# Post-LN two-layer kernel on one core: batch 0's second-layer inputs moved into the first phase's last batch, one value product moved into the first pass, the tail split by tiles

## What is computed

```python
x = _layernorm(x + _L0_attn_ref(x, Wq, bq, Wk, bk, Wv, bv, Wo))
x = _layernorm(x + _L0_ffn_ref(x, select_weight, select_mean_diff, ...))
x = _layernorm(x + _L1_attn_ref(x, Wq, Wk, Wv, Wo, bo))
x = _layernorm(x + _L1_ffn_ref(x, G, gate_w, up_w, down_w, lora_A, lora_B))

def _L1_attn_ref(x, Wq, Wk, Wv, Wo, bo):
    q, k, v = split_heads(x @ Wq), split_heads(x @ Wk), split_heads(x @ Wv)
    weights = softmax(einsum('bhqd,bhkd->bhqk', q, k) / sqrt(hd))
    ctx = einsum('bhqk,bhkd->bhqd', weights, v)
    ...
```

## Time and profile before

| | us |
|---|---|
| median of 3 runs | 739.39 |
| lowest and highest | 736.17 and 750.09 |
| the profiled execution | 738.66 |
| its span | 736.8 |
| mean granted clock of TensorE | 0.968 |
| busy: PE, DVE, ACT, POOL | 697.5, 508.7, 404.1, 106.1 |

### The profile page before, as it was taken

One profiled execution on the slowest core, in us unless ns is written; L12 is line 12 of the kernel. 1 busy time (PEld: TensorE's weight loads), 2 busy tenths in 40 slices (PEclk: granted clock), 3 DMA queues, 4 the chain that ended last, 5 costly groups with the idle time before them and its releaser, 6 DMA issues.

```text
span 736.8 us, 11487 instructions
## 1 busy us (share of the span) xinstructions
PE 697.5 (95%) x4080; PEld 483.0 (66%) x4080; DVE 508.7 (69%) x1158; ACT 404.1 (55%) x745; POOL 106.1 (14%) x116
## 2 busy tenths in 40 slices
PE   8999999999999999997899998999999999999975
PEld 5768987798878887896544543555464555546654
DVE  4666556765577656774888797869779787783463
ACT  5574356643665377552137765766548566475531
POOL 0202320132103322232202000200001000000010
PEclk9999999999999999999789999999999999999996
DMA  8300000010000020005504600252004510000000
GB/s 337 149 1 1 29 1 1 0 47 0 0 0 0 12 79 1 4 1 87 123 4 76 99 3 0 41 91 45 2 1 78 90 37 2 2 1 30 1 30 28
DMA packets 13997, 28.31 MB, mean 38 GB/s; under 512 B 2612, under 2 KB 3452, under 8 KB 13820
## 3 DMA queue, kind: packets, MB, share of 16 engines
q1 hardware_dynamic: 13084, 26.10, 14.8%
q10 hardware_dynamic: 864, 1.57, 1.3%
HBM read 12.60 MB, written 2.10 MB: 20 GB/s over the span
## 4 chain that ended last, share of the span: by engine, by line
PE 68%; DVE 18%; issue 7%; ACT 2%; DMA 2%; POOL 1%; ACTq 0%; POOLq 0%; DVEq 0%; SPq 0%
PE bank_y L414 11%; PE bank_q L355 11%; PE bank_st L1231 8%; DVE nmax L1884 7%; PE bank_c L1244 6%; PE bank_a L298 5%; PE bank_a L385 3%; PE side L1177 3%; PE side L1298 2%; PE side L1329 2%; PE bank_a L332 2%; PE bank_n L370 2%; PE side L1191 2%; PE bank_q L397 2%; PE side L1264 2%
## 5 line engine op out<-in xcount | busy, mean ns | idle before, releaser
L1884 DVE TENSOR_REDUCE nmax<-bank_s 128x1 f32<-128x512 f32 x240 | 154.2, 684 | 54.8 <-PE bank_s L1208 53.5
L1597 ACT ACTIVATE shared<-bank_st 128x512 f32<-128x512 f32 x256 | 139.0, 596 | 66.6 <-PE bank_st L1231 65.7
L1208 PE MATMUL bank_s<-ks,qs 48*128 48x512 f32 x240 | 98.6, 472 | 5.9 <-DVE nmax L1884 3.9
L1231 PE MATMUL bank_st<-qs,ks 50*128 50x512 f32 x256 | 99.1, 457 | 3.5 <-ACT shared L1597 2.6
L617 DVE SCALAR_TENSOR_TENSOR sq<-bank_q,bq,eq 128x512 f32<-128x512 f32 x64 | 47.6, 744 | 48.2 <-ACT eq L500 48.2
L414 PE MATMUL bank_y<-m_hi,s_lo 128*128 128x256 f32 x256 | 73.3, 286 | 3.1 <-POOL s_lo L250 3.1
L414 PE MATMUL bank_y<-m_hi,s_hi 128*128 128x256 f32 x256 | 72.1, 282 | 0.0
L414 PE MATMUL bank_y<-m_lo,s_hi 128*128 128x256 f32 x256 | 72.1, 282 | 0.0
L1244 PE MATMUL bank_c<-shared,v 128*32 128x512 f32 x512 | 71.6, 633 | 0.0
L250 POOL TENSOR_TENSOR s_lo<-sq,s_hi 128x512 fp32r<-128x512 f32 x32 | 42.8, 1339 | 186.1 <-ACT s_hi L505 186.1
L1231 PEld LDWEIGHTS bank_st<-qs,ks 50*128 50x128 f32 x256 | 40.2, 186 | 40.8 <-issue 21.9
(11 more groups left out here) (282 smaller groups left out, 1370.3 us busy)
## 6 DMA issues: line engine op xcount, KB each, us to landing
qs<-qk_hi SPq DMA_DIRECT2D x16, 256.0 KB, 4.9
ks<-qk_hi SPq DMA_DIRECT2D x12, 256.0 KB, 7.1
xT<-in_xT SPq DMA_DIRECT2D x4, 512.0 KB, 4.5
sq<-in_wqT SPq DMA_DIRECT2D x2, 1024.0 KB, 9.2
wo<-in_woT SPq DMA_DIRECT2D x1, 2048.0 KB, 12.9
xs<-in_x SPq DMA_DIRECT2D x1, 2048.0 KB, 17.8
qs<-qk_lo SPq DMA_DIRECT2D x8, 256.0 KB, 5.5
ks<-qk_lo SPq DMA_DIRECT2D x6, 256.0 KB, 7.2
```

The lines of the kernel that those rows point to most:

```text
L1208: pe.matmul(score_bank(b, u)[:, :], qs[part, b % 2, slot, t * P:(t + 1) * P], ks[part, b % 2, slot, :], start=True, stop=True).then_inc(s_ ...
L1231: pe.matmul(bank_st[u % 2][:, :], ks[part, b % 2, slot, kt * P:(kt + 1) * P], qs[part, b % 2, slot, :], start=True, stop=True).then_inc(st ...
L1597: act.activation(probs[:, u % SLOTS, :], bank_st[u % 2][:, :], ACT.Exp, scale=SCALE1).then_inc(p_ready, 1)
L1884: dve.tensor_reduce(nmax[:, g, t, j:j + 1], score_bank(b, u)[:, :], AX.X, ALU.max, negate=True).then_inc(max_ready, 1)
```

## The change

On TensorE `turn_x2(0, i)` moves from projections 10 and 12 to 6 and 8, both into bank "n"; `query_key(0, 0)` from 14 to 10, into bank "n"; `query_key(0, 1)` from behind the phase to projection 11. `value(0, 1)` moves from the run of scores to pair 4 of pass 0, where it takes the place of `keep_busy(0, 2)`; the context products of key tiles 0 and 1 wait for `value(0, 0)` only. VectorE's `add_update(0, 1)`, `update_stats`, `merge(2, 0)`, `x2T_rest` and `qk_rest` move up likewise, through calls of the hook behind queries 13, 14 and 15 and scale 4 that the first phase did not have; the gate work of batch 1 moves behind the first heads' maxima. ACT's and GpSimd's parts follow, ACT's transfers with them. In the tail four groups of `keep_busy` are added, and the last half's expert output, add and statistics go tile by tile, each tile into a bank of its own.

```diff
@@ first phase, VectorE
                 query(b, 13)
+                beside("query", 13)
                 query(b, 14)
                 scale(b, 2)
+                beside("query", 14)
                 scaled_lo(b, 2)
                 query(b, 15)
+                beside("query", 15)
                 scale(b, 3)
                 scale(b, 4)
+                beside("project", 4)
                 invert(b, 1)
...
+        def x2_home(b, i):
+
+            return "n" if b == 0 else i
+
+        def qk_home(b, i):
+            return ("n", 0)[i] if b == 0 and i < 2 else i % 2
...
+        LAST_OUT_AT = {2: "s1", 3: "st0"}
@@ GpSimd
-                if stage == "scaled" and n == 7:
+                if stage == "scaled" and n == 3:
                     rstd(2, 0)
+                if stage == "scaled" and n == 11:
+                    keep_x2(0)
 
             first.gpsimd(pool, beside)
-            keep_x2(0)
...
@@ TensorE
                 if s == 0:
-                    pe.wait_ge(v_ready, 2 * (b + 1))
+                    pe.wait_ge(v_ready, 2 * (b + 1) if b else 1)
+                if s == 2 and b == 0:
+                    pe.wait_ge(v_ready, 2)
                     pe.wait_ge(v_ones_ready, 1)
...
+            def expert_out_last(t):
+
+                b, home = B - 1, LAST_OUT_AT[t]
+                pe.wait_ge(hidT_ready, 3 * b + 4)
+                take(home)
+                for c in range(3):
+                    mm = pe.matmul(by_k(home)[:, 0, :], hidT[:, c, t * P:(t + 1) * P], down1[:, c, :], start=c == 0, stop=c == 2)
+                mm.then_inc(down_done, 1)
...
-                    if b == 0 and n in (2, 3, 4, 5, 10, 11):
+                    if b == 0 and n == 4:
+                        value(0, 1)
+                    if b == 0 and n in (2, 3, 5, 10, 11):
                         keep_busy(n % 2, 2)
...
+                    if n == 6:
+                        last_read["n"] = (first.den_ready, 2 * B)
+                        turn_x2(0, 0)
+                    if n == 8:
+                        turn_x2(0, 1)
                     if n == 10:
+                        query_key(0, 0)
+                    if n == 11:
                         last_read[0] = (first.m_lo_ready, maps + 7)
-                        turn_x2(0, 0)
-                    if n == 12:
+                        query_key(0, 1)
                         last_read[1] = (first.m_lo_ready, maps + 8)
-                        turn_x2(0, 1)
-                    if n == 14:
-                        query_key(0, 0)
 
             first.tensor(pe, beside)
-            query_key(0, 1)
...
-                if h == 5:
-                    value(0, 1)
...
             expert_out_half(last, 0)
+            keep_busy(0, 4)
             turn_x3(last, 1, TURN_AT[1])
+            keep_busy(0, 5)
             route(last, 1, ROUTE_AT[1])
...
+            keep_busy(1, 6)
             turn_hidden_half(last, 1)
-            expert_out_half(last, 1)
+            keep_busy(1, 3)
+            for t in (2, 3):
+                expert_out_last(t)
@@ ACT
+                    if n == 4 and b == 0:
+                        value_out(0, 1)
...
-                    if n in (9, 10):
-                        normalize(2, 0, xf, (0, 1) if n == 9 else (2, 3))
-                    if n in (12, 14):
-                        x2T_out(0, (n - 12) // 2)
+                    if n in (5, 6):
+                        normalize(2, 0, xf, (0, 1) if n == 5 else (2, 3))
+                    if n in (8, 10):
+                        x2T_out(0, (n - 8) // 2)
+                    if n in (12, 13):
+                        qk_out(0, n - 12)
+                    if n == 15:
+                        stack_rows(act, 0, 1)
 
             first.scalar(act, beside)
-            for i in range(2):
-                qk_out(0, i)
-            stack_rows(act, 0, 1)
...
@@ VectorE
+                    if n == 13:
+                        add_update(0, 1)
+                    if n in (14, 15):
+                        update_stats(0, (0, 1) if n == 14 else (2, 3))
                 if stage == "project":
-                    if n == 5:
-                        add_update(0, 1)
-                    if n == 6:
-                        update_stats(0, range(NT))
-                    if n == 7:
+                    if n == 4:
                         merge(2, 0)
-                    if n in (13, 15):
-                        x2T_rest(0, (n - 13) // 2)
+                    if n in (9, 11):
+                        x2T_rest(0, (n - 9) // 2)
+                    if n in (13, 14):
+                        qk_rest(0, n - 13)
 
             residual, residual_stats, residual_merge = first.vector(dve, beside)
-            qk_rest(0, 0)
-            normalize_x1(1, (0, 1))
-            qk_rest(0, 1)
-            normalize_x1(1, (2, 3))
+            normalize_x1(1)
             residual(B - 1)
             for i in range(2):
                 projections(1, i)
-            gate_distances(1)
-            gate_inverse(1)
-            gate_scores(1)
             for h in range(LEAD):
                 maxima(0, h, range(NT))
                 if h == 0:
+                    gate_distances(1)
+                    gate_inverse(1)
+                    gate_scores(1)
+                if h == 2:
                     gate_largest(1)
-                if h == 1:
+                if h == 3:
                     gate_pick(1)
...
-            add_experts(last, 1, OUT_AT[1])
-            expert_stats(last, 1)
+            for t in (2, 3):
+                dve.wait_ge(down_done, 2 * last + t)
+                dve.tensor_tensor(xk[:, last % 2, t, :], by_k(LAST_OUT_AT[t])[:, 0, :], xk[:, last % 2, t, :], ALU.add).then_inc(r4_ready, 1)
+                dve.wait_ge(r4_ready, 2 * last + t)
+                tile_stats(4, xk[:, last % 2], (t,))
             merge(4, last, 1)
```

More of the change, by code:

```diff
@@ L1163, in turn_x2 @@
             def turn_x2(b, i):
-                turn(xf, x2T_done, x_ready[2], b, i, i)
-                last_read[i] = (x2T_lo_ready, 2 * b + i + 1)
+                turn(xf, x2T_done, x_ready[2], b, i, x2_home(b, i))
+                last_read[x2_home(b, i)] = (x2T_lo_ready, 2 * b + i + 1)
             def query_key(b, i):
@@ L1170, in query_key @@
                 pe.wait_ge(x2T_lo_ready, 2 * (b + 1))
-                take(i % 2)
+                home = qk_home(b, i)
+                take(home)
                 first = (i % 2) * D + (i // 2) * P
@@ L1176, in query_key @@
                     for lhs, rhs in split_passes(wqkv_hi[:, k, cols], wqkv_lo[:, k, cols], x2T_hi[:, k, :], x2T_lo[:, k, :]):
-                        mm = pe.matmul(side[i % 2][:, :], lhs, rhs, start=n == 0, stop=n == 3 * KD - 1)
+                        mm = pe.matmul(banks[home][:, :], lhs, rhs, start=n == 0, stop=n == 3 * KD - 1)
                         n += 1
                 mm.then_inc(qk_done, 1)
-                last_read[i % 2] = (qk_lo_ready, 4 * b + i + 1)
+                last_read[home] = (qk_lo_ready, 4 * b + i + 1)
             def value(b, i):
@@ L1576, in x2T_out @@
                     act.wait_ge(first.sk_sum_step, (NT - 1) * B)
-                act.activation(x2T_hi[:, :, half_tokens(i)], side_k[i], ACT.Copy).then_inc(x2T_hi_ready, 1)
+                act.activation(x2T_hi[:, :, half_tokens(i)], by_k(x2_home(b, i)), ACT.Copy).then_inc(x2T_hi_ready, 1)
             def qk_out(b, i):
@@ L1581, in qk_out @@
                 at_least(act, stack_in[1 - i // 2], 16 * STACK_DMAS * (b + i // 2))
-                act.activation(qk_hi[:, i % 2, :], side[i % 2][:, :], ACT.Copy).then_inc(qk_hi_ready, 1)
+                act.activation(qk_hi[:, i % 2, :], banks[qk_home(b, i)][:, :], ACT.Copy).then_inc(qk_hi_ready, 1)
             def value_out(b, i):
@@ L1745, in _ @@
             shift_out(0, 0)
-            value_out(0, 1)
             hmT_out(1)
```

5 lines of the change are left out of this document (3 added, 2 removed).

## The result

The changed kernel took 731.55 us, median of 6 runs (730.98 to 741.12), and the kernel before 743.03, median of the 6 runs taken by then (736.17 to 750.09). The ratio is 0.989, 95% interval 0.984 to 0.994: faster, by less than 2%. The forecast was 732.0, a ratio of 0.990. The profiled execution took 730.98, its span is 729.2, and its mean granted clock 0.973 (before: 738.66, 736.8, 0.968).

What follows compares the result with a forecast made beforehand. It took TensorE as the bound nearly throughout, except in the handoff and the tail. From 738.66 us, -4.2 + 0.0 + 0.5 + 0.5 - 3.5 = -6.7 gave 732.0, range 727.5 to 739.5.

Steps and rivals of the forecast that it cites:

- The first score: Handoff moved up into the last batch's projections: first score at 343.1, -4.2 us, bounds -5.2 and -2.5.
- the merge and what stands around it: Handoff: `merge(2, 0)` ahead of `invert(1)` meets GpSimd's rest and delays the last projection by 1.25 us, bounds 0.6 and 2.0.
- The inversion: Handoff, VectorE: `invert(1)` starts 1.6 us later because the merge stands ahead of it and meets GpSimd's rest.
- Turns and copy: Handoff, behind the last projection: two turns of x1 and a copy take about 1.6 us.
- selections: Handoff: 16 selections take 1.86 us, against 3.71 at the low clock; at the low clock 1.85 later.
- the value: Handoff: `value(0, 0)` behind the selections takes 1.62 us, and TensorE is ready for the first score at 342.9.
- TensorE and the transfers would arrive within a microsecond: Handoff, ahead of the first score: TensorE ready at 342.9, transfers landed at 342.2, at worst 344.6.
- The maxima: First maxima: the gate's eight instructions add 2.26 us, VectorE's idle 2.21 goes; sum 0.0, with 0.2 either way.
- The values in the pass: First pass, pair 4: 12 value matmuls replace two fillers, +0.5 us, bounds 0 and +1.4.
- The clock at the start of the pass: Start of the first pass: without the dense value matmuls it likely starts at the low level; +0.5 us, bounds -1 and +3.
- The tail: Tail: fillers keep the clock up, add and statistics go by tiles; -3.5 us, or +0.1 if the clock falls.
- the tail stays slow: Rival: the clock falls in the tail despite the fillers, tail +0.1, total -3.1, 735.6 us; chance 0.22.

Runs made afterwards that it cites:

- merge_late: The changed kernel with `merge(2, 0)` behind `invert(1)` in the last batch's projections instead of ahead of it; median 729.26 us, ratio 0.987 against the kernel before.
- value_back: The changed kernel with `value(0, 1)` back among the first maxima and the filler back in pair 4 of the first pass; 734.52 us, ratio 0.995 against the kernel before.
- the tail alone: The kernel before with only the tail's part of the change, fillers and work by tiles; median 738.47 us, ratio 0.998 against the kernel before.
- handoff_alone: The changed kernel with the whole tail part taken back, its four groups of fillers too; median 732.58 us, ratio 0.989 against the kernel before.
- tiles_no_fill: The changed kernel without its four groups of fillers in the tail, work by tiles kept; median 733.77 us, ratio 0.990 against the kernel before.
- value_late: The changed kernel with `value(0, 0)` behind head 0's scores instead of ahead of them; median 736.72 us, ratio 0.998 against the kernel before.
- pass_less_fill: The changed kernel without the fillers of pairs 2, 3 and 5 of the first pass; median 734.52 us, ratio 0.995 against the kernel before.
- fill_lead: The changed kernel with one filler matmul behind each score of heads 1 to 7 among the first maxima; 746.54 us, ratio 1.013 against the kernel before.
- merge_value: The changed kernel with `merge(2, 0)` behind `invert(1)`, `value(0, 0)` behind head 0's scores, second products for heads 8 to 15 one head later; 731.51 us, ratio 0.989.

## Why the prediction was right, point by point

**What bounds the kernel.** As read: the handoff and the tail were the two places that gave. How much the tail gives depends on the execution that it is compared with (below).

**The first score**, -4.2 predicted (bounds -5.2 and -2.5), -4.70 measured in the chains, counted from the reciprocal (58.25 to 53.55). Its terms: the merge and what stands around it cost 1.30 (predicted 1.25; last projection 46.11 + 1.41 before, 48.82 after). The inversion came 1.48 later behind the one ahead of it (19.34 against 17.86; predicted 1.6), and merge_late gives back 0.90 of the 1.30 by moving the merge. By the Trainium skill, GPSIMD Engine Reference, Specifications, a VectorE instruction with two SBUF inputs contends with GpSimd; the pair 1.25 and 0.17 us agrees. Turns and copy took 1.22 (339.82 - 338.60; predicted 1.6), selections 2.09 (1.86) and the value 1.42 (1.62): 4.73 in all, 5.08 predicted. That TensorE and the transfers would arrive within a microsecond was right: where the value is out of the way, the transfer lands at 52.5 from the reciprocal, 1.0 ahead of the changed kernel's first score.

**The maxima**, 0.0 predicted, +0.82 measured (first score to first turned score 25.22 before, 26.04 after). The gate came between the first two heads without idle time, and the wait of 2.21 us went, as written. The step that was mis-sized is "with 0.2 either way": it counted VectorE's work alone. The last two pieces ahead of the first turned score are TensorE's, and at the low level the three fillers there take 1.65 us.

**The values in the pass**, +0.5 predicted. From pair 4's start to pair 6's the changed kernel took 8.20 us (381.16 to 389.36), before 7.79 (382.99 to 390.78): +0.41. The wait for ACT shrank from 0.70 to 0.24 us, as predicted.

**The clock at the start of the pass**, +0.5 with a bound of +3; measured +1.34 from the first turned score to pair 4's (10.45 before, 11.79 after). Right in sign and inside the bound, wrong in its reason: value_back shows the low level at the start of the pass with the values ahead of it.

**The tail**, -3.5 predicted, -3.43 measured, -3.40 with the tail alone. But this sum was made against one execution, whose clock had fallen during the last output. Against handoff_alone, with the same old tail, the same edits are worth 0.7; against tiles_no_fill the fillers alone are worth 1.0. That the term came out at -3.5 is luck in part: the profile compared with had the slow output. The rival "the tail stays slow" took for certain that the level falls in the kernel before; what the fillers do is make the best case the usual one.

**The rest.** The steps net of the start-up sum to -4.70 + 0.82 + 1.34 + 0.41 - 3.43 = -5.6; the profile shows -8.4. The rest, -2.8, lies between pair 6 and the last exponential, in code that is the same. The kernel before was at the low level there in three short stretches, near 443, 529 and 658, the changed one in one, near 588. The prediction had no term for this, and it is larger than the 2 us that it allowed to either side of its forecast. Against its sum of -6.7 stand +0.7 of start-up, -0.5 at the first score, +1.6 in maxima and pass, +0.1 in the tail and these -2.8: -7.7. The forecast of 732.0 is right partly because these went against each other. What the edits themselves are shown to give is less than the ratio of 0.989 (some 8 us): 2.1 us by exponential 20 and 0.7 to 3.4 in the tail. The rest is a better pattern of low stretches, and what in the change brings it about is not shown.

What stays open: why the clock falls near 353 with TensorE busy without a pause, and why the profiled executions of merge_late, value_late and pass_less_fill show long low stretches near 454 and 655 that the changed kernel's two do not. These executions were 4 to 9 us above the medians of their kernels, so the stretches need not be the edits'. Between exponentials 20 and 255 they took 7.3 to 9.0 us more than the changed kernel, which is more than any edit tested here gained:

```profile
651.00:673.00 22.00, 21.89 (x82) 12.73 (x83) 9.71 (x41) 9.99 (x20) 1.21 (x2) 0.61 0.07 25
```

```profile
651.00:673.00 22.00, 21.88 (x122) 12.51 (x123) 13.61 (x55) 13.67 (x29) 2.10 (x4) 1.00 0.07 25
```

The first is pass_less_fill, the second the changed kernel: 82 and 122 matmuls in the same 22 us.

## What to carry to other kernels

Count every checkpoint of two profiles from the last instruction that both share ahead of the change: the start-up then drops out, and terms of half a microsecond become readable. When a product is moved out of the way, look up who writes its bank next: most of value 0's gain of 0.8 us went into a wait for its own copy. Before a gain is read off one execution's slow stretch, ask whether the kernel always has that stretch: 12 matmuls that took 5.35 us in one profile took 2.86 in another of the same tail.

## What was not expected of the hardware

- In fill_lead the granted clock fell to 0.50 near 353, in a stretch (351 to 384) where TensorE was busy 33.00 of 33.00 us, with scores of 48 rows and fillers of 128 in turn. With fillers four in a row it fell 5 us later.
- 12 output matmuls took 2.86 us at the full level and 5.35 at the low one, in the same place of the same tail code, in different executions.
- A VectorE instruction on 128x4 took 1.25 us beside a GpSimd subtraction of 128x512 and ended with it, and 0.17 us where it stood behind it.
- Runs of one kernel (merge_value) cluster: 727.5, 731.5, 735.3 and 740.3 us at mean clocks of 0.978, 0.972, 0.966 and 0.962, some 4 to 5 us apart with nothing changed.
